# Context products of one head group at a time, or of two at once, in a float32 cross-attention kernel

## The reference

```python
q = lora(hidden, Wq, Aq, Bq)      # x @ W + 2 * (x @ A @ B); 32 heads of 32
k = lora(traces, Wk, Ak, Bk)      # 8 heads of 32, each repeated 4 times
v = lora(traces, Wv, Av, Bv)
attn = softmax(einsum('bhqd,bhtd->bhqt', q, k) / sqrt(32))
context = einsum('bhqt,bhtd->bhqd', attn, v)
out = hidden + lora(context, Wo, Ao, Bo)
```

## Time and profile before

| | us |
|---|---|
| median of 3 runs | 675.79 (675.72 to 678.38) |
| the profiled execution | 678.06 |
| its span, first to last instruction | 676.3 |
| PE busy | 662.5 (98%) |
| DVE busy | 512.7 (76%) |
| ACT busy | 467.6 (69%) |
| POOL busy | 375.9 (56%) |
| mean granted clock of PE | 0.947 |

### The profile page before, as it was taken

The page is one execution under the profiler, slowest core; times in us unless marked ns, Lnnn a source line. Parts: engine busy times, 40 slices in busy tenths (PEclk is TensorE's granted clock), DMA queues, the critical chain, the costliest instruction groups (busy, mean ns, idle before and its releaser), DMA issues.

```text
span 676.3 us, 13385 instructions
## 1 busy us (share of the span) xinstructions
PE 662.5 (98%) x4220; PEld 528.2 (78%) x4220; DVE 512.7 (76%) x1161; ACT 467.6 (69%) x1462; POOL 375.9 (56%) x325
## 2 busy tenths in 40 slices
PE   9999999999999999999999999999899999999998
PEld 6798777877877887887887788787676788888886
DVE  4768887787788778778777877878887898855542
ACT  5558888888888888888888888887678443222220
POOL 3548785843762584386358438535867005776632
PEclk9999999999999999999999999999899999999999
DMA  8956655675665567556656646667676335655331
GB/s 268 355 171 211 207 182 164 196 212 167 174 197 183 158 195 227 162 179 195 198 149 201 210 157 183 197 187 211 186 225 205 107 120 172 202 187 186 126 121 66
DMA packets 103829, 125.07 MB, mean 185 GB/s; under 512 B 9280, under 2 KB 85312, under 8 KB 103760
## 3 DMA queue, kind: packets, MB, share of 16 engines
q1 hardware_dynamic: 103760, 124.23, 59.6%
HBM read 86.18 MB, written 38.01 MB: 184 GB/s over the span
## 4 chain that ended last, share of the span: by engine, by line
PE 82%; DVE 8%; ACT 4%; DMA 3%; issue 2%; SPq 1%; DVEq 0%
PE banks L1484 20%; PE banks L1677 17%; PE banks L1482 10%; PE banks L1502 9%; PE banks L1532 8%; PE banks L1519 8%; PE banks L1543 6%; DVE neg_max L1142 2%; ACT banks L930 2%; PE banks L1463 2%; DVE turned_sb L1163 2%; DMA raw<-xt 1%; PE banks L1450 1%; DVE max_parts L1151 1%; DMA raw<-ct 1%
## 5 line engine op out<-in xcount | busy, mean ns | idle before, releaser
L930 ACT ACTIVATE banks<-banks,neg_max 128x256 f32<-128x256 f32 x512 | 229.9, 452 | 29.8 <-DVE neg_max L1142 24.6
L812 POOL TENSOR_TENSOR q_stack<-turned_sb,head_mask 8x512 fp32r<-8x512 f32 x128 | 136.0, 1062 | 172.8 <-DVE turned_sb L1163 167.1
L1142 DVE TENSOR_REDUCE neg_max<-banks 128x2 f32<-128x512 f32 x256 | 175.0, 686 | 41.9 <-PE banks L1502 38.9
L941 ACT ACTIVATE probs_t<-banks 128x512 f32<-128x512 f32 x256 | 155.0, 605 | 48.4 <-PE banks L1519 48.0
L1484 PE MATMUL banks<-x_both,w_hi 128*128 128x512 f32 x448 | 162.9, 396 | 0.1
L1482 PE MATMUL banks<-x_both,w_lo 128*128 128x256 f32 x448 | 118.6, 280 | 0.0
L1502 PE MATMUL banks<-k_stack,q_stack 96*128 96x256 f32 x512 | 109.8, 296 | 0.7 <-DMA q_stack<-q_parts 0.7
L1502 PEld LDWEIGHTS banks<-k_stack,q_stack 96*128 96x128 f32 x512 | 81.3, 190 | 35.4 <-issue 25.8
L930 ACT ACTIVATION_READ_ACCUMULATOR banks<-banks,neg_max 128x1 f32 x512 | 106.7, 208 | 0.0
L1519 PE MATMUL banks<-q_stack,k_stack 104*128 104x512 f32 x256 | 102.4, 400 | 0.0
L1482 PEld LDWEIGHTS banks<-x_both,w_lo 128*128 128x128 f32 x448 | 84.5, 189 | 9.2
(11 more groups left out here) (156 smaller groups left out, 1154.7 us busy)
## 6 DMA issues: line engine op xcount, KB each, us to landing
q_stack<-q_parts SPq DMA_DIRECT2D x192, 128.0 KB, 3.0
q_parts<-q_stage SPq DMA_DIRECT2D x64, 256.0 KB, 3.5
raw<-ct SPq DMA_DIRECT2D x32, 256.0 KB, 3.5
raw<-xt SPq DMA_DIRECT2D x32, 256.0 KB, 3.8
scales<-r_rows SPq DMA_DIRECT2D x64, 128.0 KB
context<-ctx_stage SPq DMA_DIRECT2D x64, 128.0 KB, 3.7
stage<-xn SPq DMA_DIRECT2D x16, 512.0 KB, 5.4
w_hi<-context SPq DMA_DIRECT2D x14, 512.0 KB, 7.0
```

Of the source, the lines that this page charges most:

```text
L812: nc.gpsimd.tensor_tensor(q_stack[rows, u % RING, heads], turned_sb[rows, u % 2].unsqueeze(1).broadcast_to([M_ROWS, 2, S]), head_mask[rows ...
L930: last = nc.scalar.activation(score_bank(s)[:, S * h:S * (h + 1)], score_bank(s)[:, S * h:S * (h + 1)], ACT.Exp, bias=neg_max[:, u % 2, i: ...
L941: nc.scalar.activation(probs_t[:, u % 2, t, 2 * hp:2 * hp + 2, :].rearrange("p a b -> p (a b)"), st_bank[j % 2], ACT.Exp, scale=-1.0).then ...
L1142: nc.vector.tensor_reduce(out=neg_max[:, u % 2, 2 * c:2 * c + 2], in_=score_bank(s).rearrange("p (h t) -> p h t", h=2), axis=AXIS, op=ALU. ...
```

## The change

Context products are made for two units at once. In the first slot of every odd unit `u`, `context_pair` takes units `u - 3` and `u - 2`: four products side by side (32 output columns each), two heads of one unit each with 512 moving columns, where `context` had one head with 256. The last slot of the odd unit normalizes both at once from the whole bank, with 512 columns (`normalize_pair`). The even units have neither. This holds for the units below `PAIRED` = 54 (27 pairs); the last ten go singly as before.

Since the first unit of a pair waits a unit longer for its product, the transposed probabilities get a third buffer (the room of `w_sum`, free between the weight preparation and the last batch). Rows of the context come out in another order (two heads of two groups in one store), and Wo's and Ao's rows are laid in that order on the host.

The reciprocals of a group are spread to 64 partitions by 512 columns: `put_rows` writes its four rows so that the two heads of a partition block lie side by side, and `spread` reads 2 rows of 2 KB, each copied to 32 partitions, where it read 4 rows of 1 KB, each copied to 32. On SP's list `spread(g)` now stands right behind `put_rows(g + 1)`, and the stores of the context are two in a row (`store_pair`), behind the even groups' spreads.

```diff
+PAIRED = NB * NG - NG - 2
...
+        p_room = [probs_t[:, 0], probs_t[:, 1],
+                  w_sum[:].rearrange("p a b -> p (a b)").rearrange("p (t h n) -> p t h n", t=2, h=GH)]
...
+        def contexts_before(n):
+            if n >= PAIRED:
+                return n - 1
+            return n - 1 if n % 2 else n - 2
...
+                def store_pair(g):
+                    if first and g < 0:
+                        return
+                    wait(ctx_done, unit0 + (g + 2))
+                    v, n = place_of(g)
+                    for i in range(2):
+                        sp.dma_start(ctx_dram[v, n + i], ctx_stage[:, i]).then_inc(ctx_stored[i], DMA)
...
                 def put_rows(g):
                     wait(turned_out, unit0 + (g + 2))
-                    sp.dma_start(r_dram[g % 2], turned_sb[KM:KM + GH, (g + 1) % 2]).then_inc(r_stored[g % 2], DMA)
+                    rows = r_dram[g % 4]
+                    if unit0 + g < PAIRED:
+                        rows = rows.rearrange("(j h) n -> h j n", h=2)
+                    sp.dma_start(rows, turned_sb[KM:KM + GH, (g + 1) % 2]).then_inc(r_stored[g % 2], DMA)
 
                 def spread(g):
                     if first and g < 0:
                         return
                     wait(r_stored[g % 2], b * (4 * DMA) + DMA * (g // 2 + 1))
+                    if unit0 + g < PAIRED:
+                        need(sp, ctx_done, unit0 + (g - g % 2))
+                        rows = P // 2 * (g % 2)
+                        sp.dma_start(scales[rows:rows + P // 2].rearrange("p a n -> p (a n)"),
+                                     r_dram[g % 4].rearrange("(j h) n -> j (h n)", h=2).unsqueeze(1).broadcast_to([2, HD, 2 * S])
+                                     ).then_inc(r_spread[g % 2], DMA)
+                        return
                     need(sp, ctx_done, unit0 + (g - 1))
-                    sp.dma_start(scales[:, g % 2], r_dram[g % 2].unsqueeze(1).broadcast_to([GH, HD, S])
+                    sp.dma_start(scales[:, g % 2], r_dram[g % 4].unsqueeze(1).broadcast_to([GH, HD, S])
...
                 stack_q(4, fills + 3, st0 + 4)
                 put_rows(1)
+                spread(0)
+                store_pair(-2)
                 load_x(1)
                 send(pos["q", 5, 0])
                 load_x(2)
-                spread(1)
                 send(pos["q", 6, 0])
-                store_ctx(0)
                 stack_q(5, fills + 3, st0 + 8)
                 put_rows(2)
+                spread(1)
                 load_x(3)
-                spread(2)
                 send(pos["q", 7, 0])
-                store_ctx(1)
                 stack_q(6, fills + 4, st0 + 12)
+                put_rows(3)
+                spread(2)
+                store_pair(0)
                 load_context(b + 2, 0)
-                put_rows(3)
                 load_context(b + 2, 1)
+                send(pos["k", 0, 1])
                 load_context(b + 2, 2)
-                send(pos["k", 0, 1])
-                spread(3)
                 load_context(b + 2, 3)
-                store_ctx(2)
                 send(pos["k", 1, 1])
                 stack_q(7, fills + 4, st0 + 16)
                 put_rows(4)
+                spread(3)
                 stack_k(0, b + 2, st0 + 16)
-                spread(4)
...
+            def normalize_pair(b, u):
+                for i in range(2):
+                    dve.wait_ge(r_spread[i], b * (4 * DMA) + DMA * (u // 2 + 2))
+                    dve.wait_ge(ctx_stored[i], b * (4 * DMA) + DMA * (u // 2 + 1))
+                dve.wait_ge(ctx_mm, b * NG + (u + 2))
+                nc.vector.tensor_tensor(ctx_stage[:].rearrange("p a n -> p (a n)"), ctx_bank,
+                                        scales[:].rearrange("p a n -> p (a n)"), ALU.mult).then_inc(ctx_done, 2)
...
-                if c == 3 and not (first and u < 2):
-                    normalize(b, u - 2)
+                if c == 3:
+                    if b * NG + u - 2 >= PAIRED:
+                        normalize(b, u - 2)
+                    elif u % 2 and b * NG + u - 3 >= 0:
+                        normalize_pair(b, u - 3)
...
+            def context_pair(b, u):
+                need(pe, ctx_done, b * NG + u)
+                pe.wait_ge(st_exp, b * SLOTS + (4 * u + 8))
+                if u == 0:
+                    pe.wait_ge(v_moved, b + 1)
+                for t in range(2):
+                    for k in range(4):
+                        g, j = u + k // 2, k % 2
+                        last = nc.tensor.matmul(
+                            ctx_bank[HD * k:HD * (k + 1), :].rearrange("p (h n) -> p h n", h=2),
+                            v_sb[:, t, HD * (g % NG):HD * (g % NG + 1)],
+                            p_buf(b * NG + g)[:, t, j::2, :], start=(t == 0), stop=(t == 1),
+                            tile_position=(0, HD * k))
+                last.then_inc(ctx_mm, 2)
...
-                if c == 0 and not (first and u < 2):
-                    context(b, u - 2)
+                if c == 0:
+                    if b * NG + u - 2 >= PAIRED:
+                        context(b, u - 2)
+                    elif u % 2 and b * NG + u - 3 >= 0:
+                        context_pair(b, u - 3)
```

More of the change, by code:

```diff
@@ L171, in xattn @@
         t1_raw, t2_raw = (probs_t[:, i].rearrange("p a b n -> p (a b n)").rearrange("p (a n) -> p a n", a=4)
-                          for i in range(2))
+                          for i in (1, 0))
+        p_room = [probs_t[:, 0], probs_t[:, 1],
+                  w_sum[:].rearrange("p a b -> p (a b)").rearrange("p (t h n) -> p t h n", t=2, h=GH)]
         t4_raw = t1_raw
@@ L185, in xattn @@
         k_dram = nc.dram_tensor("k_parts", [2, 2, P, S], F32, kind="Internal").ap()
-        r_dram = nc.dram_tensor("r_rows", [2, GH, S], F32, kind="Internal").ap()
+        r_dram = nc.dram_tensor("r_rows", [4, GH, S], F32, kind="Internal").ap()
         ctx_dram = nc.dram_tensor("context", [NB, NG, P, S], F32, kind="Internal").ap()
@@ L518, in body, with place_of @@
                 fills = b * 4
+                def place_of(g):
+                    return (b, g) if g >= 0 else (b - 1, g + NG)
                 def store_ctx(g):
+                    wait(ctx_done, unit0 + (g + 1))
+                    v, n = place_of(g)
+                    rows = P // 2 * (n % 2)
+                    sp.dma_start(ctx_dram[v, n - n % 2:n - n % 2 + 2, rows:rows + P // 2],
+                                 ctx_stage[:, g % 2]).then_inc(ctx_stored[g % 2], DMA)
+                def store_pair(g):
                     if first and g < 0:
                         return
-                    wait(ctx_done, unit0 + (g + 1))
-                    row = ctx_dram[b, g] if g >= 0 else ctx_dram[b - 1, g + NG]
-                    sp.dma_start(row, ctx_stage[:, g % 2]).then_inc(ctx_stored[g % 2], DMA)
+                    wait(ctx_done, unit0 + (g + 2))
+                    v, n = place_of(g)
+                    for i in range(2):
+                        sp.dma_start(ctx_dram[v, n + i], ctx_stage[:, i]).then_inc(ctx_stored[i], DMA)
                 def load_x(*chunks):
@@ L556, in body @@
                     return
-                spread(-1)
-                store_ctx(-2)
                 stack_q(3, fills + 2, st0)
@@ L561, in body @@
                 put_rows(0)
+                spread(-1)
                 load_x(0)
                 send(pos["q", 4, 0])
-                spread(0)
-                store_ctx(-1)
                 stack_q(4, fills + 3, st0 + 4)
                 put_rows(1)
+                spread(0)
+                store_pair(-2)
                 load_x(1)
@@ L591, in body @@
                 put_rows(4)
+                spread(3)
                 stack_k(0, b + 2, st0 + 16)
-                spread(4)
                 send(pos["q", 0, 1])
-                store_ctx(3)
                 stack_q(0, fills + 5, st0 + 20)
                 put_rows(5)
+                spread(4)
+                store_pair(2)
                 send(pos["q", 1, 1])
-                spread(5)
-                store_ctx(4)
                 send(pos["q", 2, 1])
@@ L603, in body @@
                 put_rows(6)
-                spread(6)
+                spread(5)
                 send(pos["q", 3, 1])
-                store_ctx(5)
                 stack_q(2, fills + 6, st0 + 28)
                 put_rows(7)
+                spread(6)
+                store_pair(4)
                 if b == NB - 2:
@@ L1176, in normalize @@
                 dve.wait_ge(ctx_stored[u % 2], b * (4 * DMA) + DMA * (u // 2 + 1))
-                nc.vector.tensor_tensor(ctx_stage[:, u % 2, :], ctx_bank, scales[:, u % 2, :],
+                nc.vector.tensor_tensor(ctx_stage[:, u % 2, :], ctx_bank[:, 0:S], scales[:, u % 2, :],
                                         ALU.mult).then_inc(ctx_done, 1)
+            def normalize_pair(b, u):
[5 more added lines that the diff above has]
```

(4 more changed lines are left out.)

25 lines of the change are left out of this document (16 added, 9 removed).

## The result

The changed kernel takes 794.35 us (median; 791.93 to 794.85) against 677.0 of the kernel before in the same job, a ratio of 1.1736, 95% interval 1.1717 to 1.1755. So it is slower, as forecast, but by 117 us and not by 28: far outside the range of 680 to 718.

A forecast was written before the change was run, and what follows sets the result against it. PE, busy 98% of the span, bounds the kernel; after the change a loop through DVE, SP and the spread sets the pace: 26 loops of 410.5 us against 382.2, so 675.8 + 28 = 704 us, range 680 to 718.

The forecast's parts named there:

- What a pair costs PE: PE's context products: a pair takes 2.11 us in place of 2.44, so 27 pairs save 8.8 us.
- The loop and its engine: Normalization, DVE's list, turn, put_rows, spread, normalization: forecast loops of 14.2 to 17.7 us; DVE waits, PE loses its pace.
- SP loses its waits for the landing of rows, which is a gain for the loads behind: SP's list: fewer waits for r_rows; counted with normalization width, third buffer and context stores as nothing together.
- The sum: 26 loops between first and last pair: 410.5 us against 382.2 before, so 28 us slower.
- The spread's 5.2: Reciprocals' DMA into scales: 5.2 us taken, between 4.35 by the row's rate and 6.05 with half the engines.
- The lower bound: Spread's landing if it keeps the rate seen for four source rows: 4.35 us.
- The argument against the halving: New spread on two engines, not four, by the skill page's rule; longer pieces were held against the full 6.05 us.
- Issues of SP at 0.4: SP's list between turn and spread: issuing put_rows takes 0.34 us, with gaps 0.4.
- The last ten units and the output part are as before: Stretch behind the last pair, units done singly: no change in time.
- Half the engines in full: Rival on the spread's transfer: 6.05 us, loops 49 us more, 725 us in all; chance 0.08.
- the spread keeps its rate: Rival on the spread's transfer: 4.35 us, loops 11 or 5 us more, between them 684 us; chance 0.20.
- it lands before it is needed: Faster rival: spread landing after 3.0 us, most of the 8.8 us kept, some 6 us, 670 us; chance 0.12.

The follow-up runs named there:

- form undone: Changed kernel, each paired spread as two transfers of one source row to 32 partitions, place and pairs unchanged: 697.89 us, ratio 1.0302.
- repaired kernels: Changed kernel with one-row spread transfers (697.89 us), also odd groups' spreads earlier on SP's list (688.96), also single context stores as two of 64 rows (681.02); later edits build on these.
- both: Changed kernel, odd groups' spreads earlier on SP's list and each paired spread as two one-row transfers, pairs kept: 688.96 us, ratio 1.0168.
- two hidden limits: Changed kernel with early one-row spreads and 64-row stores, plus two context loads moved later and one input's low part moved from DVE to GpSimd: 672.65 us.
- place 39: Kernel before, every spread right behind the next group's put_rows, still one transfer of four rows: 717.16 us, ratio 1.0582.
- form 91: Kernel before, each spread as two transfers of two rows at the old place, no pairs: 769.29 us, ratio 1.1336.
- place undone: Changed kernel, odd groups' spreads three to five entries earlier on SP's list, two rows outermost as in the change: 737.11 us, ratio 1.0866.

## Why the prediction was wrong in its size

- *What a pair costs PE: right.* By the marks of the earlier trace rows, on PE's timeline of the changed kernel:

```profile
288.86 0.40 PE L1566 MATMUL banks<-q_stack,k_stack 104*128 104x512 f32 x1
...
290.40 0.39 PE L1566 MATMUL banks<-q_stack,k_stack 104*128 104x512 f32 x1
...
292.21 0.40 PE L1566 MATMUL banks<-q_stack,k_stack 104*128 104x512 f32 x1
...
295.80 0.40 PE L1566 MATMUL banks<-q_stack,k_stack 104*128 104x512 f32 x1
```

  A slot is 1.54, one with a pair 3.59 (the slot between them holds a wait of 0.3), so a pair costs 2.05; 2.11 was forecast from 4 x 0.448 + 0.32. What makes up the 0.32 no run took apart.
- *The loop and its engine: right.* DVE waits at the pair's normalization for the scales, PE behind it, and PE's saving is lost. DVE's list fits within 0.1 for three of four loops (11.5 from 3 to 5); from 7 to 1 it is 9.2 in place of 8.6.
- *"SP loses its waits for the landing of rows, which is a gain for the loads behind", put with others at nothing: the step that failed.* SP's waits for `r_rows` did fall, from 81 to 19 us. But the step priced the new form of the spread for the spread alone. Other transfers share its engines; the sends land after 5.3 us in place of 3.5, `stack_q` waits for them on SP's list, and `put_rows` stands behind it. The sum has `put_rows` late in unit 5 alone, by 0.6, and nothing for the other units; it is 3.0 and 2.2 late in units 3 and 7. That is 32 of the 76 us by which the loops were under-sized. The run with `put_rows` moved ahead of `stack_q` gives back 35 us, 32 of them in the loops. Not all of the lateness in unit 3 is the slow sends': with the form undone 1.8 is left there, and 0.05 in unit 7. And nothing was no value from a row: in the kernel before, `put_rows` starts 1.6, 0.5, 1.3 and 1.7 us behind the turn in units 1, 3, 5 and 7 (means of seven batches), of which only unit 5's was read.
- *The spread's 5.2: too small,* by as much, 32 us. The middle between 4.35 and 6.05 was taken. From its issue to the normalization it is 6.44 on average: the spreads land after 6.15 (5.2 to 7.1 by the trace's landing events), near the upper bound, and 0.29 pass from the landing to the normalization, which the sum left out. The lower bound was right for four rows, and needn't have been reckoned: by the landing events of the trace before, which the page doesn't list for it, a spread lands after 4.18 (median). The argument against the halving, that the pieces are longer, had no row behind it. The rule of the Trainium skill, page "DMA: Bandwidth & Descriptors", which was given a chance of 0.08, was right.
- *Issues of SP at 0.4: 0.70,* 8 us. `put_rows` as a store with a transposed pattern takes 0.60 in place of 0.34.
- *"The last ten units and the output part are as before": wrong by 6 us,* most of it the single stores' new form (undoing it took 5.3 us off that stretch), and the first pair is 5.45 late where 2 was taken.
- *The rivals.* "Half the engines in full" was the right mechanism with 725 us and not enough, since it too charged only the spread. The repaired kernels move towards "the spread keeps its rate" (684) and "it lands before it is needed" (670): 698 with the form undone, 689 with both, and 672.65 once the stores' form and two hidden limits are cleared.

So place and form don't add up. In the kernel before: place 39, form 91. In the changed one: place undone 57 less, form undone 96 less, both 105. In the changed kernel each makes the same loop long, and the form also makes SP's list and PE's query stacks late.

## What to carry to other kernels

A transfer with few rows outermost is to be priced twice: for its own landing, and for every other transfer whose last part queues behind it on the engines that it holds; then follow each of those to the waits on the issuing queue. Two transfers that run on all engines can be far cheaper than one that runs on two (698 against 794 us here). And where a change takes work off the engine that sets the pace, list what had been just fast enough behind it: here two limits together took back some 10 us in seven batches, and clearing either alone showed 2 to 3.

## What the runs showed of the hardware beyond that

- The form of the spreads didn't touch all transfers alike: the median landing of `q_stack` is 2.6 to 3.0 us in every kernel here, that of the query sends goes from 2.5 to 5.5. Why was not tried.
- An input's low part on DVE, 0.68 us in the earlier trace rows, lasts up to 1.5 right behind a pair's normalization in unit 3 of the repaired kernels (0.7 to 1.5 by batches), while GpSimd works on the next inputs' high parts. It is one of the steps that make DVE late in unit 4. Why it lasts so long there wasn't tried.

```profile
309.34 0.64 DVE L1225 TENSOR_TENSOR ctx_stage<-banks,scales 128x512 f32<-128x512 f32 x1
309.89 1.52 DVE L1231 TENSOR_TENSOR x_both<-raw,x_both 128x512 fp32r<-128x512 f32 x1
```
